# Attention stages of a transformer on one core: the row of maxima sent first, three part transfers a set, fewer loads at the start, single-head score banks, and projections in two halves

## The reference

```python
x = x + _L0_attn_ref(_layernorm(x), ...)   # block mask: blocks of 32, masked scores are 0
x = x + _L0_ffn_ref(_layernorm(x), ...)    # fp4 quantized
x = x + _L1_attn_ref(_layernorm(x), ...)   # causal, with a linear bias by distance
x = x + _L1_ffn_ref(_layernorm(x), ...)    # ternary
x = x + _L2_attn_ref(_layernorm(x), ...)   # full attention
x = x + _L2_ffn_ref(_layernorm(x), ...)
x = x + _L3_attn_ref(_layernorm(x), ...)   # state space block
x = x + _L3_ffn_ref(_layernorm(x), ...)

# block attention
q = (h @ Wq.T + bq).reshape(B, S, NUM_HEADS, HEAD_DIM)     # k, v alike
scores = jnp.einsum('bihd,bjhd->bhij', q, k) / scale
scores = jnp.where(blk[:, None] >= blk[None, :], scores, 0)
probs = jax.nn.softmax(scores, axis=-1)
ctx = jnp.einsum('bhij,bjhd->bihd', probs, v).reshape(B, S, H)
return ctx @ Wo.T + bo
```

## Time and profile before

| | |
|---|---|
| runs | 2164.28, 2164.27, 2430.3 us; median 2164.28 |
| profiled execution | 2159.32 us, its span 2157.5 us |
| granted TensorE clock | 0.923 mean |
| busy in the span | PE 84%, PEld 38%, DVE 60%, ACT 49%, POOL 33% |
| costliest groups | maxima L686 534 us of DVE; Exps L586 349 and L579 275 us of ACT; L330 230 and L352 227 us of PE |

### The profile page before, as it was taken

How to read it: one execution, slowest core, us unless ns; L and a number is a source line. 1 busy time by engine, 2 the same in 40 slices (tenths; PEclk the granted TensorE clock), 3 DMA queues, 4 the chain that set the end, 5 groups by cost and what they waited for, 6 DMA issues and landing times.

```text
span 2157.5 us, 33272 instructions
## 1 busy us (share of the span) xinstructions
PE 1821.9 (84%) x11885; PEld 817.1 (38%) x11885; DVE 1288.2 (60%) x3442; ACT 1048.2 (49%) x1768; POOL 712.6 (33%) x796
## 2 busy tenths in 40 slices
PE   2788788765648888888999999899999967999998
PEld 0233333233433444444445454233233234444443
DVE  1666667727776776775101111898899826776663
ACT  1266566541213665666232232488788844445432
POOL 2166766455451232220111110133322025444320
PEclk9799989877787999999999999799999978999999
DMA  7332334000013234430000002232334010000000
GB/s 195 72 60 60 74 79 84 1 17 1 0 45 74 60 72 88 80 61 2 2 0 1 0 0 59 59 60 60 72 84 83 2 49 1 0 11 5 6 10 10
DMA packets 70269, 91.71 MB, mean 43 GB/s; under 512 B 13228, under 2 KB 63644, under 8 KB 65228
## 3 DMA queue, kind: packets, MB, share of 16 engines
q1 hardware_dynamic: 64680, 84.69, 18.8%
q10 hardware_dynamic: 5424, 4.89, 0.7%
HBM read 49.30 MB, written 39.85 MB: 41 GB/s over the span
## 4 chain that ended last, share of the span: by engine, by line
PE 54%; issue 6%; DVE 4%; ACT 3%; DMA 2%; SPq 1%; POOL 1%; DVEq 0%; ACTq 0%; POOLq 0%
PE ps L1421 5%; PE ps L410 5%; PE ps L1433 4%; PE ps L2853 3%; PE ps L384 3%; PE ps L368 3%; PE ps L1398 3%; PE ps L396 3%; PE ps L2134 2%; PE ps L2136 2%; PE ps L2152 2%; PE ps L352 2%; PE ps L330 2%; DMA Qst<-mT 2%; ACT Pr L579 1%
## 5 line engine op out<-in xcount | busy, mean ns | idle before, releaser
L686 DVE TENSOR_REDUCE mx<-ps 128x1 f32<-128x512 f32 (+3 forms) x1024 | 534.4, 583 | 151.1 <-PE ps L352 116.4
L586 ACT ACTIVATE Pr<-ps 128x1024 f32<-128x1024 f32 (+3 forms) x512 | 348.5, 706 | 223.8 <-PE ps L330 113.1
L579 ACT ACTIVATE Pr<-ps 128x512 f32<-128x512 f32 x512 | 274.5, 601 | 50.1 <-PE ps L384 44.8
L352 PE MATMUL ps<-Kst,Qst 63*128 63x512 bf16 (+3 forms) x1024 | 227.1, 327 | 61.0 <-DVE mx L686 26.6
L330 PE MATMUL ps<-Qst,Kst 64*128 64x512 bf16 (+3 forms) x1024 | 229.8, 327 | 56.6 <-issue 37.8
L682 DVE CUSTOM_DVE_ANT_0 vs<-ps,cT 128x512 f32<-128x512 f32 (+3 forms) x512 | 225.7, 488 | 84.7 <-PE ps L352 81.6
L2881 POOL TENSOR_TENSOR ve<-mv,eps 128x4 f32<-128x4 f32 x41 | 8.7, 213 | 626.8 <-DVE mv L2870 626.8
L368 PE MATMUL ps<-Pr,V 128*32 128x512 f32 (+3 forms) x2048 | 208.0, 481 | 4.6 <-ACT ctxU L592 3.1
L396 PE MATMUL ps<-Kst,Qst 63*128 63x512 bf16 x512 | 170.0, 403 | 5.5 <-DVE mx L686 3.3
L410 PE MATMUL ps<-Pr,V 128*32 128x256 f32 x2048 | 164.6, 393 | 8.6 <-ACT ctxU L592 7.6
L384 PE MATMUL ps<-Qst,Kst 64*128 64x512 bf16 x512 | 154.4, 386 | 17.8 <-issue 10.2
(11 more groups left out here) (340 smaller groups left out, 3265.7 us busy)
## 6 DMA issues: line engine op xcount, KB each, us to landing
Qst<-parts_scratch SPq DMA_DIRECT2D x48, 384.0 KB, 5.5
Kst<-parts_scratch SPq DMA_DIRECT2D x48, 384.0 KB, 8.2
parts_scratch<-qpart SPq DMA_DIRECT2D x48, 192.0 KB, 2.7
parts_scratch<-kpart SPq DMA_DIRECT2D x48, 192.0 KB, 2.7
parts_scratch<-qpart SPq DMA_DIRECT2D x48, 128.0 KB, 2.6
parts_scratch<-kpart SPq DMA_DIRECT2D x48, 128.0 KB, 2.7
parts_scratch<-qpart SPq DMA_DIRECT2D x48, 64.0 KB, 2.3
parts_scratch<-kpart SPq DMA_DIRECT2D x48, 64.0 KB, 2.3
```

The source lines that it names most:

```text
L352: mm = pe.matmul(ps[:, 4 + a, lo:lo + W], k.Qst[rows, n.par, pair, P * it:P * it + P], k.Kst[rows, n.par, pair, 0:W], start=True, stop=True)
L579: act.activation(k.Pr[:, g % 2, 2 * (j // 2) + 1 - j % 2, :], ps[:, self.bank_t(b, g, j), :], ACT.Exp).then_inc(self.s_exp.sem, 1)
L586: act.activation(k.Pr[:, g % 2, 2 * tile:2 * tile + 2, 0:W], ps[:, 2 * tile:2 * tile + 2, 0:W], ACT.Exp).then_inc(self.s_exp.sem, 1)
L686: dve.tensor_reduce(k.mx[:, half, at:at + 1], ps[:, bank, lo:lo + W], AX_X, ALU.max, negate=True).then_inc(self.s_max.sem, 1)
```

## The change

The diff has five parts.

1. `STACKING` is permuted, so that one transfer of 128 partitions writes a block of parts: 3 for q and 3 for k where there were 6 and 6. The stacks are still read by 2 transfers each.
2. SP: the row of maxima goes first at slot 6, then q parts, k parts at slot 7, the stacks at 8. POOL: k is split directly behind q, ahead of `context(prev, 2)`. The transpose of the maxima stands inside slots 6 and 14, behind the third head.
3. Start: ACT issues 5 loads (ident, the biases and weights of q and k), then 7 more, and waits for the 5; the other 31 are issued by SP at slot 8 of frames 0, 1 and 2. DVE waits only for X, POOL for its own fills, PE for the 5 loads, SP for nothing. What else needs first loads waits for them later (`prepared`, slot 10 of frame −1).
4. Stages 0 and 2 use `head_t`, `head_m` and `half_pv` as stage 4 does: one head to a bank, three banks for transposed scores and three for fills, four Exps of 128 x W a slot for two of 128 x 2W, pv in two column halves where W is over 128. The separate order for odd and even slots is gone.
5. q and k projections, values and outputs go in two halves, one behind the slot's third head, one at its end; in all three stages.

```diff
-STACKING = (np.arange(P) % 8 * 2 + np.arange(P) // 64) * DH + np.arange(P) // 8 % 8
+STACKING = (np.arange(P) % 8 * 2 + np.arange(P) // 8 % 2) * DH + np.arange(P) // 16
...
+            pe.wait_ge(self.s_max.sem, self.s_max.at(n, self.taken(fill - 2)))
+            for it in its:
+                W, lo = self.span(it), self.place(its, it)
+                mm = pe.matmul(ps[:, self.bank_m(n, fill), lo:lo + W], k.Qst[rows, n.par, pair, P * it:P * it + P],
+                               k.Kst[rows, n.par, pair, 0:W], start=True, stop=True)
...
+            W = self.width(jt)
+            first, last = T - W, T
+            cuts = (first, (first + last) // 2, last) if W > P else (first, last, last)
+            lo, hi = cuts[half:half + 2]
...
+        def project(n, step, half):
+            cols = slice(half * T // 2, (half + 1) * T // 2)
+            w, ready, done = ((self.w["q"], self.s_xnT, self.s_q_ps), (self.w["k"], self.s_q, self.s_k_ps))[step - 3]
+            if half == 0:
+                pe.wait_ge(ready.sem, ready.at(n))
+            mm = pe.matmul(misc[:, cols], w, k.xnT[:, cols], start=True, stop=True)
+            if half == 1:
+                mm.then_inc(done.sem, 1)
...
+                for j in range(4):
                     if b.valid():
+                        head_t(b, g, j)
                     if mb.valid():
+                        head_m(mb, c, j)
+                    if j in (1, 3) and pb.valid():
+                        half_pv(pb, pg, j // 2)
+                    if j == 2 and s in (6, 14):
+                        row_statistics(f, s)
+                    if j == 2:
+                        misc_first(f, s)
                 misc_step(f, s)
...
-            for tile in range(2):
-                act.wait_ge(self.s_scores_t.sem, self.s_scores_t.at(b, 2 * g + tile + 1))
-                if tile == 0:
+            for j in range(4):
+                act.wait_ge(self.s_scores_t.sem, self.s_scores_t.at(b, 4 * g + j + 1))
+                if j == 0:
                     act.wait_ge(self.s_pv.sem, self.s_pv.at(b, g - 1))
-                act.activation(k.Pr[:, g % 2, 2 * tile:2 * tile + 2, 0:W],
-                               ps[:, 2 * tile:2 * tile + 2, 0:W], ACT.Exp).then_inc(self.s_exp.sem, 1)
+                act.activation(k.Pr[:, g % 2, 2 * (j // 2) + 1 - j % 2, 0:W],
+                               ps[:, self.bank_t(b, g, j), 0:W], ACT.Exp).then_inc(self.s_exp.sem, 1)
...
-            if block and prev.valid():
-                context(prev, 2)
-            early(f, 2)
-            if f.c != 0 and n.valid():
                 pool.wait_ge(self.s_k.sem, self.s_k.at(n))
                 pool.wait_ge(self.s_split.sem, self.s_split.at(n, 4))
                 pool.wait_ge(self.s_k_out.sem, self.s_k_out.at(n.plus(-1)))
                 split(n, k.kf[:, :], k.kpart, 4)
             if block and prev.valid():
+                context(prev, 2)
+            early(f, 2)
...
-            for a in range(2):
-                rows = slice(64 * a, 64 * a + 64)
-                if j == 0:
-                    for lo, hi, p in QBLOCKS:
-                        sp.dma_start(k.scratch[0, a, lo:hi].rearrange("b r t -> r b t"),
-                                     k.qpart[rows, p, :].unsqueeze(1).broadcast_to([64, hi - lo, T]))\
-                          .then_inc(self.s_q_out.sem, 16)
...
+            if j == 0:
+                for lo, hi, p in QBLOCKS:
+                    sp.dma_start(k.scratch[0, lo:hi].rearrange("b r t -> r b t"),
+                                 k.qpart[:, p, :].unsqueeze(1).broadcast_to([P, hi - lo, T]))\
+                      .then_inc(self.s_q_out.sem, 16)
...
-                if s in (5, 7) and nxt.valid():
-                    part_out(nxt, (s - 5) // 2)
+                if s == (5 if f.c == -1 else 6) and nxt.valid():
+                    part_out(nxt, 0)
+                if s == (5 if f.c == -1 else 7) and nxt.valid():
+                    part_out(nxt, 1)
...
+                if s == 8 and not self.opened and 0 <= f.c < 3:
+                    k.load_weights(sp, f.c)
...
+            for dst, src in k.start_loads:
+                act.dma_start(dst, src).then_inc(k.s_start_weights, 16)
...
+            act.wait_ge(k.s_start_weights, 16 * len(k.start_loads))
```

More of the change, by code:

```diff
@@ L271, in fills @@
             sets = ((0, 2), (1,)) if phase else ((3,),)
-        u = 8 * pair + 2 * sum(len(its) for its in self.first_sets()) * phase
+        at = 2 * phase * (1 if self.causal else 2)
         out = []
@@ L392, in head_m @@
+            a, fill, its = fills[i]
             rows = slice(64 * a, 64 * a + MROW)
-            if u == 0:
+            if fill == 0:
                 pe.wait_ge(self.s_stacked.sem, self.s_stacked.at(n))
-            pe.wait_ge(self.s_max.sem, self.s_max.at(n, u - 2))
-            pe.matmul(ps[:, self.bank_m(n, u), :], k.Qst[rows, n.par, pair, P * it:P * it + P],
-                      k.Kst[rows, n.par, pair, :], start=True, stop=True).then_inc(self.s_scores.sem, 1)
+            pe.wait_ge(self.s_max.sem, self.s_max.at(n, self.taken(fill - 2)))
@@ new lines, in rows, with values, outputs, misc_first @@
+        def rows(src, w, half):
+            for t in (2 * half, 2 * half + 1):
+                mm = pe.matmul(misc[:, P * t:P * t + P], src[:, P * t:P * t + P], w, start=True, stop=True)
+            return mm
+        def values(half):
+            return rows(k.xnT, self.w["v"], half)
+        def outputs(half):
+            return rows(k.ctxT, self.w["o"], half)
+        def misc_first(f, s):
+            prev, nxt = f.plus(-1), f.plus(1)
+            n, step = projecting(f, s, self.opened)
+            if step in (3, 4) and n.valid():
+                project(n, step, 0)
+            if s == 10 and nxt.valid() and not (self.opened and f.c == -1):
+                if f.c == -1:
+                    k.prepared(pe)
+                pe.wait_ge(self.s_cT_read.sem, self.s_cT_read.at(prev))
+                pe.wait_ge(self.s_mT.sem, self.s_mT.at(f, 1))
+                pe.wait_ge(self.s_k.sem, self.s_k.at(nxt))
+                values(0)
+            if s == 12 and prev.valid() and self.kind != "full":
+                pe.wait_ge(self.s_c2.sem, self.s_c2.at(prev))
+                outputs(0)
@@ L669, in maxima @@
             half, i = divmod(pair, 4)
-            for a, u, its in fills:
+            for a, fill, its in fills:
+                u = self.taken(fill)
                 dve.wait_ge(self.s_scores.sem, self.s_scores.at(n, u + len(its)))
@@ L677, in maxima @@
                     at = 16 * a + 4 * i + it
-                    bank = self.bank_m(n, u) if self.kind == "full" else 4 + a
+                    bank = self.bank_m(n, fill)
                     if self.kind == "alibi":
```

271 lines of the change are left out of this document (90 added, 181 removed).

## The result

The changed kernel takes 2127.85 us (median of 4, 2122.17 to 2132.35) where the kernel before takes 2164.28; the ratio is 0.984, 95% interval 0.980 to 0.987. That is 36 us, or 1.6%, where 104 us were forecast. The ratio leaves out the one execution of the kernel before that took 2430.3 us, which ran in a slower state of the chip. The profiled execution took 2132.35 us, its span 2130.6 us, with a mean granted clock of 0.926 for 0.923. The two profiled executions lie only 27 us apart.

What follows compares the result with a forecast made beforehand. TensorE plus its waits was taken to bound the masked stages. Start −26, stage 0 −38, stage 2 −26, stage 4 −6, halves −6 made −102: 2057 from the profiled 2159.3, about 2060 as median; range from 6 below 2024 to 2110.

Steps and rivals of the forecast that it cites:

- The start: At the kernel's start, VectorE needs X alone; the first fill comes at 32.7 instead of 58.97 us, counted as 26 us.
- SP's order: At slot 8, row of maxima sent first; with three transfers, stage 0 gains 14 us, stage 2 13 and 3, stage 4 6.
- three transfers: On SP, three issues take about 2.0 us where six took 3.91; the gain is counted together with SP's order.
- POOL's order: On POOL, k split ends 4.4 us earlier; stage 0's 6.8 us wait for the keys' stack goes, counted as 6.
- the clock: Behind the slot 8 wait, TensorE's half-clock stretches go: 8 us gained in stage 0 and 5 in stage 2.
- half of the maxima waits: In stages 0 and 2, single heads over 3+3 banks remove 10 of 21.2 and 5 of 10.4 us of waits.
- halves, net: Pv and projections in halves keep ACT's Exps fed: net gain 0.4 a batch in stages 0 and 2, 6 us.
- the upper bound: In stages 0 and 2, added pv weight loads cost at most 0.22 us each, 42 us over 192 second pvs.
- Rival C: Half of pv's 42 us on TensorE's path; maxima waits, clock, halves give nothing: 2115, range 2095 to 2135; chance 0.20.
- The prediction's own sign: A batch in stage 0 over 44 us means forecast wrong, waits moved to slot 14's fill or to Exps.
- Read-Write Bubble: Skill's rule for 512 to 1024 element tiles on ScalarE: by it alone, single heads' Exps lose up to 88 us.
- semaphore tail: Skill's 26.3 ns for each increment: two more a slot over 256 slots would add 13 us; no row shows it.

Runs made afterwards that it cites:

- order_start: Kernel before plus lean start, new SP and POOL order, three transfers a set; transpose's place, head pairs, whole pv and projections as before: 2084.9 us, repeated 2086.5.
- pool_old: order_start with the context step ahead of the k split on POOL again: 2117.7 us, ratio 0.980.
- six_parts: order_start with the old six transfers a set, 64 partitions each: 2147.5 us, ratio 0.992.
- row_in_slot: order_start with the transpose of the maxima inside slots 6 and 14: 2077.3 us, ratio 0.961.
- singles_together: singles_alone with the two heads of a pair scored next to each other, no fill between them: 2093.3 us, ratio 0.968.
- singles_alone: Changed kernel with whole projections, values and outputs, and whole pv in the masked stages: 2096.5 us, ratio 0.969.
- halves_adjacent: Changed kernel with q, k, values and outputs still in two pieces, both at the slot's end: 2102.5 us, ratio 0.973.
- whole_pv: Changed kernel with pv of the masked stages in one piece behind the second head: 2113.8 us, ratio 0.977.
- whole_proj: Changed kernel with q, k, values and outputs in one piece at the slot's end: 2103.7 us, ratio 0.974.

## Why the prediction was wrong

*Point by point, what held.* The start was put at 26 us: the first fill came 21.8 earlier and the first Exp 24.5. X landed at 3.91, earlier than the 5.8 of the earlier trace rows allowed, but q parts were issued at 21.03, 2.3 us behind their split, for which no row shows a reason, and the keys' stack took 10 us to its release and not 6.4. SP's order, three transfers, POOL's order and the clock were put at 28, 21 and 6 us in the three stages: `order_start` shows 29.7, 19.3 and 5.8. `pool_old` and `six_parts` show POOL's order and the three transfers each by a wait of its own; SP's order by itself is not shown to gain. The clock, put at 8 and 5 us, fits TensorE's 8 and 7 us of lower busy time in `order_start`. The sum of the prediction without parts 4 and 5 is 81, and 78 and 84 were measured, with the transpose at the end of its slot and inside it.

*What failed are the two terms of parts 4 and 5.* They stood at −15 (half of the maxima waits) and −6 (halves, net). Measured: the single heads with the order of pieces that came with them +16 (`row_in_slot` to `singles_together`), the fill between heads +3 (not clear of noise), both kinds of halves +31 (`singles_alone` to the changed kernel). That is +50 where −21 stood, 71 us; the first three parts gave 3 more than their sum, and the forecast missed by 68. The halves are shown by `halves_adjacent` and `whole_pv`; what of the 16 us is single heads and what the place of the transpose stays open.

*The step behind them* is that TensorE's work was taken as fixed by its columns, and the cost of a split was put at nothing. For pv the upper bound was 0.22 us a split, 42 in all, worked out from a weight load of 108 ns. It was near the truth, 0.19 us and 37, but a net gain was chosen because the loads might lie beside running matmuls. For the projections no price was set at all, only the gain of feeding ACT; a piece parted around a score group took 0.30 us more. But the earlier trace rows say that TensorE is the busiest engine in both stages, and a step that adds a turn to the busiest engine should have been priced as on the path. Rival C said so: 2095 to 2135, and the time lies inside it. It got 0.20, and the range was cut at 2110, about its middle. Its sum, 2115, comes near the time partly by luck: it gave up the clock and the maxima waits, of which `order_start` and the changed kernel show that they came, and took only half of pv's price.

*The maxima waits* did fall by 10 us in stage 0 as forecast, and went altogether in stage 2, but falling waits of an engine are worth something only if its work stays the same. The prediction's own sign, a batch of stage 0 over 44 us, came: 44.9 by the starts of the q projections (89.3 to 313.7 us over five batches). Its reading of that sign, waits moved to slot 14 or to Exps, did not hold; the waits fell, and TensorE's work grew.

*The clock* hardly came back in stage 0 of the changed kernel (0.91 granted for 0.90). It still has a stretch at the lower level behind slot 8, though TensorE waited only 0.73 us there, and `order_start` has none:

```profile
191.00:194.00 3.00, 2.58 (x21) 0.69 (x23) 1.80 (x6) 2.12 (x6) 2.82 (x4) 0.50 1.10 327
```

```profile
189.00:194.00 5.00, 4.66 (x39) 1.75 (x37) 3.65 (x9) 4.17 (x7) 4.92 (x8) 1.00 1.09 288
```

Over stage 0 the granted clock is 0.91 in the changed kernel, 0.94 in `order_start` and in `whole_proj`, 0.90 in `whole_pv`. So part of what `whole_proj` gives back in stage 0 is clock. Why the one dips and the other doesn't was not tried. The clock thus moves with nearly every edit of this study, and the prices of single edits in stages 0 and 2 hold it in them; in stage 4 it is 0.99 or 1.00 in all runs.

*What the Exps cost.* Of the Trainium skill's Read-Write Bubble ("Advanced Engine Details and Errata") the prediction said that by it the single heads would lose up to 88 us of ACT time. ACT's busy time rose from 223 to 246 us in stage 0 and from 207 to 229 in stage 2, 44 us and not 88: Exps that follow each other overlap, and two of 128 columns take 0.42 us together in `singles_together`, where one takes 0.28. By that sign the trace agrees with the page in direction only. ACT is not the bound in these stages (246 of 366 us), but TensorE does wait for its copy of bank 6, 5 us in stage 2 of `singles_together` where `row_in_slot` has no such wait. The Trainium skill's semaphore tail ("TensorE: Matmul & The Clock Gate", The cost: per-tile semaphore tail) was put at 13 us; no run here separates it.

## What to carry to other kernels

Before a piece of work is cut in two to fill gaps, ask which engine runs it: on the busiest one each piece put between others costs a turn (0.30 us here for a projection parted around a score group), while two pieces side by side cost nothing. A queue order that sends the urgent transfer first can merely move the lateness to what was ahead of it, as with six transfers here; look at the next thing that the queue owes, and shorten the issue as well. When a slot's pieces change places, follow also the small one that a transfer hangs on, here the transpose of the maxima, and count the work that is left to cover its way. And where several edits come in one change, sum them in two groups, those that remove a wait and those that add an instruction on the bounding engine, and let the range reach over the whole of the case in which the second group costs its price.

## What was not expected of the hardware

Issuing a transfer of 128 partitions and twice the bytes takes SP hardly longer than one of 64: 3 in 1.73 us for q, where 6 took 3.91, and 3 in 2.24 for k, where 6 took 3.90. With everything else equal, six for three cost some 60 us, in the start and the three stages. And matmul groups of one kind that follow each other directly run partly into each other: four score matmuls of 512 columns in 0.54 us together, two in 0.31 when other work comes behind them.
